# Fewer partitions to a transfer and four blocks to a matmul: the output and node features of a four-layer graph network

## The reference, cut to what matters

```
m = concat([x[row], x[col], edge_attr]); h = relu(m @ W1 + b1); h = relu(h @ W2 + b2); h = h @ W3 + b3
agg_mean, agg_max = segment mean and maximum of h over col        # 32 wide each
o = concat([x, agg_mean, agg_max, u[batch]])                      # 64 + 32 + 32 + 32, u the same for all nodes
o = relu(o @ W4 + b4); o = relu(o @ W5 + b5); out = o @ W6 + b6   # 160 -> 32 -> 32 -> 64
x = layernorm(x + out)
```

## Time and profile before

| | us |
|---|---|
| three runs | 13070.82, 13071.3, 13152.06 |
| median of the runs | 13071.3 |
| profiled execution, its own time | 13160.62 |
| its span | 13158.9 |
| GpSimd busy | 9662.0 (73%) |
| VectorE busy | 6175.8 (47%) |
| TensorE busy | 2819.3 (21%) |
| mean granted TensorE clock | 0.558 of full speed |

### The profile page before, as it was taken

One profiled execution on the slowest core, in us unless ns is written; L12 is line 12 of the kernel. 1 busy time (PEld: TensorE's weight loads), 2 busy tenths in 40 slices (PEclk: granted clock), 3 DMA queues, 4 the chain that ended last, 5 costly groups with the idle time before them and its releaser, 6 DMA issues. The chain is left out here.

```text
span 13158.9 us, 78994 instructions
## 1 busy us (share of the span) xinstructions
PE 2819.3 (21%) x12129; PEld 1989.0 (15%) x12156; DVE 6175.8 (47%) x21573; ACT 1273.1 (10%) x3641; POOL 9662.0 (73%) x10101
## 2 busy tenths in 40 slices
PE   2000011111100740000000000013444444444446
PEld 2000011111100420000000000012232332332233
DVE  8877357777733432222222222224555555555554
ACT  3111011111110320000000000000000000001011
POOL 7777757777777747777777777777777777777774
PEclk6555555555555665555555555555666666666665
DMA  5444334444443332222222222222222222222221
GB/s 168 119 118 115 108 106 118 117 116 118 115 119 108 124 103 66 65 66 64 67 64 67 64 67 64 67 51 55 66 66 66 66 64 66 65 66 66 66 66 32
DMA packets 731549, 1103.24 MB, mean 84 GB/s; under 512 B 240731, under 2 KB 347192, under 8 KB 730567
## 3 DMA queue, kind: packets, MB, share of 16 engines
q0 software_dynamic: 332944, 306.83, 12.6%
q1 hardware_dynamic: 231478, 567.25, 11.4%
q10 hardware_dynamic: 167040, 228.30, 5.7%
HBM read 548.64 MB, written 552.93 MB: 84 GB/s over the span
## 5 line engine op out<-in xcount | busy, mean ns | idle before, releaser
L130 POOL DMA_INDIRECT msg<-Y,idx x3125 | 2965.9, 949 | 1060.1 <-issue 951.8
L130 POOL DMA_INDIRECT g<-in_edge_attr,idxs x3072 | 2948.7, 960 | 1017.7 <-issue 858.3
L130 POOL DMA_INDIRECT yg<-ytab,idx x3125 | 2951.8, 945 | 962.4 <-issue 950.0
L1520 DVE SCALAR_TENSOR_TENSOR run<-run,same,msg 128x64 f32<-128x64 f32 x3125 | 890.7, 285 | 3030.5 <-DMA msg<-Y,idx 2923.0
L584 DVE SCALAR_TENSOR_TENSOR run<-run,sameD 128x80 f32<-128x80 f32 x3072 | 906.3, 295 | 1396.9 <-DMA g<-in_edge_attr,idxs 875.2
L1914 DVE SCALAR_TENSOR_TENSOR run<-run,same,ps 128x32 f32<-128x32 f32 x3125 | 774.9, 248 | 1640.7 <-PE ps L1808 1538.0
L1108 PE MATMUL ps<-tail,before 128*128 128x64 f32 (+2 forms) x10 | 2.8, 422 | 4575.7 <-PEq L1422 3931.0
L1897 DVE SCALAR_TENSOR_TENSOR zx<-zx,same,zs 128x32 f32<-128x32 f32 x3124 | 792.1, 254 | 136.7 <-DVE anew L1880 29.1
L588 DVE SCALAR_TENSOR_TENSOR runS<-runS,sameS,g 128x64 f32<-128x64 f32 x3072 | 850.3, 277 | 0.0
L1789 PE MATMUL ps<-eaT,W1e 128*128 128x512 f32 (+1 forms) x394 | 401.6, 1123 | 1962.7 <-DMA yg<-ytab,idx 1962.1
L952 PE MATMUL ps<-hot 128*98 128x128 bf16 x3072 | 373.1, 315 | 1891.0 <-DVE hot L680 1891.0
(11 more groups left out here) (339 smaller groups left out, 6217.2 us busy)
## 6 DMA issues: line engine op xcount, KB each, us to landing
R<-run SPq DMA_DIRECT2D x390, 320.0 KB, 2.3
R<-run SPq DMA_DIRECT2D x195, 512.0 KB, 2.7
R<-run SPq DMA_DIRECT2D x124, 800.0 KB, 3.8
v<-in_edge_attr ACTq DMA_DIRECT2D x384, 256.0 KB
RA<-runS SPq DMA_DIRECT2D x256, 256.0 KB, 3.0
Y<-tab SPq DMA_DIRECT2D x98, 512.0 KB, 2.7
msg<-Y,idx POOLq DMA_INDIRECT x3125, 2.4
Z<-zeros SPq DMA_DIRECT2D x125, 400.0 KB, 4.3
```

Of the source, the lines that this page charges most:

```text
L130: eng.indirect_dma_start(out=out, out_offset=None, in_=table, in_offset=bass.IndirectOffsetOnAxis(ap=index, axis=0)).then_inc(sem, 16)
L1520: ins_ = v.scalar_tensor_tensor(out=run[:, q, t, :], in0=prev, scalar=same[:, q, t:t + 1], in1=msg[:, q, t, :], op0=ALU.mult, op1=ALU.add)
```

## The change

- The transfers that move 127 partitions of `X` are each made two: partitions 0 to 111 (MOSTP = 112) and 112 to 126 (15 of them). This holds for the load (L790) and for the three cuts of the output (L1991).
- In `nodes_3`, the hidden rows of four pairs of blocks are stacked on the partitions: stack j (32 partitions) holds blocks 2j and 2j + 1, in 256 columns; `h1`, `h2` become 128 x 256. W4 stands in a zeroed 128 x 224 tile, of which a window of 128 columns puts its result on the partitions of stack j; four such matmuls (of 256, 256, 128 and 256 columns) add up in one bank. W5 is a block diagonal of four copies: one matmul of 256 columns. W6 lies four times, once to a stack: three matmuls of 192, 192 and 64 columns for the seven blocks. One ScalarE instruction takes the place of two behind W4 and behind W5.
- Three more weight tiles are zeroed by GpSimd, the wait before the weight loads counts nine, and the list of loads grows from 38 to 55 small transfers.

```diff
-            sp.wait_ge(wzero, 6)
+            sp.wait_ge(wzero, 9)
...
-            sp.dma_start(k.X[0:LASTP, :, :], ins["x"][0:LASTP * NB, :].rearrange("(p b) f -> p b f", b=NB)).then_inc(settled, 16)
+            for a, z in ((0, MOSTP), (MOSTP, LASTP)):
+                sp.dma_start(k.X[a:z, :, :], ins["x"][a * NB:z * NB, :].rearrange("(p b) f -> p b f", b=NB)).then_inc(settled, 16)
...
-                sp.dma_start(most[:, a:z, :], k.X[0:LASTP, a:z, :]).then_inc(saved, 16)
-                saves += 1
+                for i, j in ((0, MOSTP), (MOSTP, LASTP)):
+                    sp.dma_start(most[i:j, a:z, :], k.X[i:j, a:z, :]).then_inc(saved, 16)
+                    saves += 1
...
-                for b in range(GB):
-                    last = nc.tensor.matmul(psY[q][:, b * D:(b + 1) * D], h2[:, b * P:(b + 1) * P], k.W6[:, :],
-                                            start=False, stop=b == GB - 1)
-                last.then_inc(outp, 1)
+                both = psY[q][:, 0:(GB - 1) * D].rearrange("p (j c f) -> p j c f", c=2, f=D)
+                nc.tensor.matmul(both[:, :, 1, :], h2[:, P:2 * P], k.W6e[:, 0:STACK - 1, :], start=False, stop=False)
+                nc.tensor.matmul(both[:, :, 0, :], h2[:, 0:P], k.W6e[:, 0:STACK - 1, :], start=False, stop=False)
+                nc.tensor.matmul(psY[q][:, (GB - 1) * D:], h2[:, 0:P], k.W6e[:, STACK - 1, :], start=False, stop=True)\
+                    .then_inc(outp, 1)
...
-                    for i, (a, z) in enumerate(halves):
+                    for i, stacks in enumerate(((0, 1), (3, 2))):
                         pe.wait_ge(turned_c, 2 * g + i + 1)
-                        nc.tensor.matmul(psH[:, a:z], k.W4a[:, :], catT[:, a:z], start=True, stop=True).then_inc(hid, 1)
+                        for j in stacks:
+                            n = min(2, GB - 2 * j) * P
+                            last = nc.tensor.matmul(psH[:, 0:n], k.W4z[:, (STACK - 1 - j) * MSG:(2 * STACK - 1 - j) * MSG],
+                                                    catT[:, 2 * j * P:2 * j * P + n], start=j == 0, stop=j == 2)
+                    last.then_inc(hid, 1)
...
-                    for a, z in halves:
-                        nc.tensor.matmul(psH2[:, a:z], k.W5[:, :], h1[:, a:z], start=True, stop=True).then_inc(hid2, 1)
+                    nc.tensor.matmul(psH2, k.W5e[:, :], h1[:, :], start=True, stop=True).then_inc(hid2, 1)
...
-                    for i, (a, z) in enumerate(halves):
-                        act.wait_ge(hid, 2 * g + i + 1)
-                        last = act.activation(h1[:, a:z], psH[:, a:z], ACT.Relu, bias=ub[:, 0:1])
-                    last.then_inc(hid_r, 1)
+                    act.wait_ge(hid, g + 1)
+                    act.activation(h1[:, :], psH, ACT.Relu, bias=ub[:, 0:1]).then_inc(hid_r, 1)
...
+            k.loads += [(k.W4u[:, j, :], w("W4")[HID:, :]), (k.b4[d, :], col(w("b4"))), (k.W5e[d, d], w("W5")), (k.b5[d, :], col(w("b5"))),
+                        (k.W6e[d, j, :], w("W6"))]
```

More of the change, by code:

```diff
@@ L19 @@
 LASTN = N - LASTP * NB
+MOSTP = LASTP // 16 * 16
+STACK = P // 32
 D = 64
@@ L812, in _ @@
                 sp.wait_ge(storedS[q], 16 * C2)
-            sp.wait_ge(settled, 16 * (NW + 5 + 2 + 6))
+            sp.wait_ge(settled, 16 * (NW + 5 + 3 + 6))
         @block.gpsimd
@@ L849, in _ @@
             pool.memset(k.b1z[:, :], 0.0).then_inc(wzero, 1)
+            pool.memset(k.W4z[:, :], 0.0).then_inc(wzero, 1)
+            pool.memset(k.W5e[:, :], 0.0).then_inc(wzero, 1)
+            pool.memset(k.W6e[:, :, :], 0.0).then_inc(wzero, 1)
             pool.memset(k.ones[:, :], 1.0).then_inc(wzero, 1)
@@ L1959, in nodes_3 @@
         catT = sb("catT3", [P, GB * P])
-        h1 = sb("nh1", [MSG, GB * P])
-        h2 = sb("nh2", [MSG, GB * P])
+        h1 = sb("nh1", [P, 2 * P])
+        h2 = sb("nh2", [P, 2 * P])
         y = sb("y3", [P, GB, D])
@@ L1966, in nodes_3 @@
         std = sb("std3", [P, GB])
-        ub = sb("ub3", [MSG, 1])
+        ub = sb("ub3", [P, 1])
         rows_got = [sem(f"rows_got3{q}") for q in range(2)]
@@ L1971, in nodes_3 @@
                              "outp3", "nsteps3", "var3", "root3", "ubs3", "ub_ready3", "y_ready3", "saved"))
-        psT, psH, psH2 = k.psf[:, 0:GB * P], k.psf[0:MSG, 1024:1024 + GB * P], k.psf[0:MSG, 2048:2048 + GB * P]
+        psT, psH, psH2 = k.psf[:, 0:GB * P], k.ps[:, 2, 0:2 * P], k.ps[:, 4, 0:2 * P]
         psY = [k.ps[:, 6 + q, 0:GB * D] for q in range(2)]
@@ L2010, in _ @@
         def _(pe):
-            nc.tensor.matmul(k.ps[0:MSG, 7, 0:1], k.W4u[:, :], k.u3[:, :], start=True, stop=True).then_inc(ubs, 1)
+            nc.tensor.matmul(k.ps[:, 7, 0:1], k.W4u[:, :, :].rearrange("p j f -> p (j f)"), k.u3[:, :], start=True,
+                             stop=True).then_inc(ubs, 1)
             def turn_rows(g, q):
@@ L2066, in body @@
                     g = 2 * c + q
-                    for i, (a, z) in enumerate(halves):
-                        act.wait_ge(hid, 2 * g + i + 1)
-                        last = act.activation(h1[:, a:z], psH[:, a:z], ACT.Relu, bias=ub[:, 0:1])
-                    last.then_inc(hid_r, 1)
+                    act.wait_ge(hid, g + 1)
+                    act.activation(h1[:, :], psH, ACT.Relu, bias=ub[:, 0:1]).then_inc(hid_r, 1)
                     if ahead or q == 0:
                         take_rows(g + 1)
[L2073 to L2076, removed]
+                    act.wait_ge(hid2, g + 1)
+                    act.activation(h2[:, :], psH2, ACT.Relu, bias=k.b5[:, 0:1]).then_inc(hid2_r, 1)
                     if later(c, q):
@@ L2080, in _ @@
             act.wait_ge(ubs, 1)
-            act.activation(ub[:, :], k.ps[0:MSG, 7, 0:1], ACT.Identity, bias=k.b4[:, 0:1]).then_inc(ub_ready, 1)
+            act.activation(ub[:, :], k.ps[:, 7, 0:1], ACT.Identity, bias=k.b4[:, 0:1]).then_inc(ub_ready, 1)
             act.wait_ge(ub_ready, 1)
@@ L2179, in build @@
                                             sb("b2e", [P, 1]), sb("b3", [P, MSG]))
-        k.W4a, k.W4u, k.u3, k.b4 = sb("W4a", [HID, MSG]), sb("W4u", [MSG, MSG]), sb("u3", [MSG, 1]), sb("b4", [MSG, 1])
-        k.W5, k.b5, k.W6, k.b6 = sb("W5", [MSG, MSG]), sb("b5", [MSG, 1]), sb("W6", [MSG, D]), sb("b6", [1, D])
+        k.W4z, k.W4u = sb("W4z", [HID, (2 * STACK - 1) * MSG]), sb("W4u", [MSG, STACK, MSG])
+        k.u3, k.b4 = sb("u3", [MSG, 1]), sb("b4", [P, 1])
+        k.W5e, k.b5, k.W6e, k.b6 = sb("W5e", [P, P]), sb("b5", [P, 1]), sb("W6e", [P, STACK, D]), sb("b6", [1, D])
         def w(name, n=3):
@@ L2198, in build @@
             (k.b3[:, :], row(w("b3")).to_broadcast([P, MSG])),
-            (k.W4a[:, :], w("W4")[0:HID, :]), (k.W4u[:, :], w("W4")[HID:, :]), (k.u3[:, :], w("u")[0:1, :].rearrange("a n -> n a")),
-            (k.b4[:, :], col(w("b4"))), (k.W5[:, :], w("W5")), (k.b5[:, :], col(w("b5"))), (k.W6[:, :], w("W6")), (k.b6[:, :], row(w("b6"))),
+            (k.W4z[:, (STACK - 1) * MSG:STACK * MSG], w("W4")[0:HID, :]), (k.u3[:, :], w("u")[0:1, :].rearrange("a n -> n a")),
+            (k.b6[:, :], row(w("b6"))),
         ]
```

## The result

| | before | after |
|---|---|---|
| median of the runs, us | 13071.3 | 12910.15 |
| lowest to highest | 13070.82 to 13152.06 | 12906.58 to 12933.84 |
| profiled execution's span | 13158.9 | 12932.1 |

The ratio of the runs is 0.9865 (95% interval 0.9826 to 0.9905). By medians the kernel is 161.2 us faster; the forecast was 152.4 less, 12919. The two profiled executions are 226.8 us apart, 74 more than the sum, and that has to be explained as well as the 161.

The account below looks back on a forecast made before the run. GpSimd was taken to bound the three edge stages and TensorE nodes_3. Savings of 80.2 (load of X), 47.2 (end) and 25 us (nodes_3), 152.4 in all, off 13071.3 gave 12919 us, range 12902 to 13003.

Parts of the forecast that it names:

- nodes_3: Last node stage: stacking shortens TensorE's steps; 25 us saved, bounds 12 and 30.
- the sum: All three gains together: 80.2 + 47.2 + 25 = 152.4 us off the 13071.3 us median.
- the low end of the range: Whole kernel: 12902 us, from 80.2 + 48 + 30 giving 12913 and some us for the scatter.
- The load of X: First edge stage: the split load removes GpSimd's hole and takes 7.4 us; 80.2 us saved, bounds 74 and 80.2.
- The end: After VectorE's last instruction: split output cuts leave 3.7 us against 50.9; 47.2 us saved, bounds 43 and 48.
- TensorE would go on setting the pace: nodes_3: TensorE takes 10.6 us a group against 12.6, so 127 us for the stage.
- The weight loads: TensorE in nodes_3: 95 ns per 128-column load, added to W4 (3.9 us) and W5 (1.1 us).
- the limit of 30: nodes_3: GpSimd's 98 gathers take 125 us, then 15 us of TensorE's pass among others; no more than 30 us saved.
- No hole in the shorter runs: Rival on the load of X: the load was quick there, only 72.2 us to gain, 12999 us; chance 0.14.
- nodes_3 gains nothing: Rival: the VectorE-GpSimd index loop or added loads take its gain; 127.4 us saved, 12944 us; chance 0.10.
- One engine still: Rival on the transfers of X: 112 and 15 partitions use one engine as 127 did; 13059 us; chance 0.03.
- Slower by the weight loads: Rival in SyncE's queue: 17 added loads delay the stores, slower from 21.6 us each, 13214 at 30; chance 0.03.

Follow-up runs that it names:

- e1: Kernel before with only the load of X split into 112 and 15 partitions: 12984.87, 12990.85, 13016.69 and 15079.15 us, ratio 0.9937.
- e2: Kernel before with only the three cuts of the output split into 112 and 15 partitions: 13022.55 us, ratio 0.9965.
- e16: Kernel before, unchanged, profiled again on a chip of the ordinary speed: profiled span 13064.0 us.
- e18: Kernel after with W5 and output of group 12 put before group 13's transposes in the last turn of nodes_3: 12906.32 and 12909.36 us, ratio 0.988.
- e5: Kernel after with X loaded as 124 and 3 partitions instead of 112 and 15: median of two runs 12930.06 us.
- e4: Kernel after without the stacking and its weight loads, both transfers of X still split: 12943.39 us, ratio 0.9901.
- e3: Kernel after with both transfers of X back at 127 partitions, so the stacking and its weight loads alone: 13052.24 us, ratio 0.9984.
- e8: Kernel after with 36 more small weight loads into tiles that nothing reads: 12932.65 and 12933.87 us.
- e9: Kernel before, unchanged, profiled once more, on a chip where every kernel took a fifth more: 15786.17 us, nodes_01 695.5 us.

## Why the prediction was right or wrong

Two things failed: the size of one term, nodes_3, for which I took 25 us and at most 30 and the runs show 30 to 33; and the low end of the range, 12902, in which I gave next to nothing to the difference between executions of before, 81 to 107 us in its long ones.

**The load of X** was right in mechanism and size: 80.2 us of hole in GpSimd, and none in after; by e1's runs 80.8 us. edges_01 lost 68.0 us from e2 to e1 (3988.1 to 3920.1) and 77.1 from e16 to e18 (3986.2 to 3909.1), where I gave 74 to 80.2. What is missing in the first pair is the gathers' pace: e1's 3072 were busy 2962.1 us against e2's 2950.3, and in the second pair, of like pace, nearly nothing is missing. The load itself took 15 us and not 7.4. The error was in giving sixteen engines sixteen times the rate of one; it stayed hidden, as GpSimd's lead covers it; e5 shows that at 4 engines it no longer does in full.

**The end** gave 47.5 against 47.2 in the profiles and 49.1 by e2's runs, by the row of the 256 and 512 KB stores.

**nodes_3** is the term that was mis-sized: 33.0 us in the profiles, 33 by runs between e4 and after, where I took 25 and called 30 the most. The stage without stacking has a spread of its own, 179.6 and 179.8 us in before and e2 but 176.6 to 176.9 in e1, e4 and e16, so that 30 to 33 is what is shown. The step of the prediction that failed is that TensorE would go on setting the pace, at 10.6 us a group and 127 us in all; it was busy 92 us, and GpSimd's 125.4 us set it.

Two prices were off. The weight loads: I took 95 ns for each from W6's 64-column passes and added them to W4 and W5. In after, W5's two passes of 256 columns start at 12877.87 and W4's at 12878.73, 0.86 us later in a stretch at 1.2 GHz, which is the 512 columns alone at 1.7 ns; W4's eight passes took 12869.69 to 12872.66, 2.97 us, less than the 3.12 of before. The seven transposes of the same group, of 128 columns and a load each, took 12867.28 to 12868.83, 0.22 us each, again the columns alone. So what I had read as a load behind 64 columns isn't seen behind 128 or 256; that was my bound, not my value. That the rest in the 64-column passes is the load stays a reading; no run takes it apart. And TensorE's pass behind the last gather, which I put at 15 us on the way to the limit of 30, took 10.0, to 12922.26. The chain of after (start us, us, what) and the last output and last update:

```profile
12912.29 0.99 PE ps L2026 x7
12913.28 0.61 PE ps L2059 x2
12913.89 3.08 PE ps L2050 x8
12916.97 0.94 PE ps L2035 x2
12917.91 0.52 PE ps L2038 x2
12918.43 0.33 PE ps L2039 x2
```

```profile
12921.73 0.53 PE L2040 MATMUL ps<-W6e,nh 128*128 128x64 f32 x2
12923.87 0.62 DVE L2127 TENSOR_TENSOR y<-ps,X 128x448 f32<-128x448 f32 x1
```

VectorE starts the last group's update 1.6 us after that output, because the update of the group before, 4.8 us long, stands in front; this takes back a part (in e18's order too, 1.8 us). The bias and outputs of the chain go at 0.94 and about 1.0 us, at a granted clock of 1.00, the 2.4 GHz level (W4 before them at 0.52). I had priced this pass at 1.2 GHz, the level of the earlier trace rows, where TensorE has no gaps, in a kernel in which by my own sum it would have gaps. That GpSimd's 98 gathers would take 125 us was right to 0.4 us.

**What the sum left out** was nodes_01, and here the range failed rather than the sum. I took the 89 us between the profiled execution and the median as a constant under all stages, and the 81 us between runs as either noise or the hole. By the profiles the 89 us are the length of one stage, nodes_01, whose code the change doesn't touch; the 81 us have no profile. The low end of the range allowed 11 us below the sum of the largest gains (12913 to 12902), and a single long execution on the side of before (one of its runs, 13152.06) takes the ratio from 0.988 to 0.9865: 12895 us if laid on 13071.3, below the 12902 that I gave. The median of after itself, 12910.15, lies inside. The trace of before could have shown it: nodes_01's window has TensorE busy 423 of 532 us at a granted clock of 0.68, so TensorE is busy for four fifths of a stage and between its two levels; that it could also run at 0.84 that trace alone doesn't say.

**The rivals.** No hole in the shorter runs: wrong by e1, whose quick runs are 80.8 us below before's, and by e16. nodes_3 gains nothing: wrong, though e3 shows 19.5 us if the end isn't freed. One engine still: wrong by after's DMA share. Slower by the weight loads: they take 0.4 us each from a wait of 200 (e8).

## What to carry to other kernels

Look at the DMA share while nothing else runs: a steady 1/16 says that one engine carries a transfer, and a partition count of 127 is enough for it. Such a transfer cost 80 us where stores followed on its queue, and at the end it hid a part of TensorE's gain (19.5 us where 33 were to be had). Price a weight load by how long the matmul beside it is, price TensorE at both clock levels when the change gives it gaps (nodes_3 was at 0.56 to 0.58 without them and at 0.71 to 0.81 with them on the ordinary chips), and before reading a difference between two executions, compare the stages that the change doesn't touch.

## What I had not expected of the hardware

- All sixteen engines moved 213 to 279 GB/s together with the gathers, where one alone had moved 27.
- The same stage of the same kernel took 445 or 532 us by TensorE's granted clock (0.84 or 0.68).
- On two chips the kernel before had medians of 15648 and 15786 us, against 13064 to 13086 elsewhere. VectorE's dependent steps were 1.40 us apart there, where a gather leaves every 1.25 us on the others and VectorE keeps up: in e9's timeline of edges_2 each waits 1.11 us behind the one before it. What makes such a wait so long there stays open.

```profile
7005.40 0.28 DVE L1520 SCALAR_TENSOR_TENSOR run<-run,same,msg 128x64 f32<-128x64 f32 x1 [1.11 <-DVE run L1520]
7006.80 0.28 DVE L1520 SCALAR_TENSOR_TENSOR run<-run,same,msg 128x64 f32<-128x64 f32 x1 [1.11 <-DVE run L1520]
```
